# Perceiver layer on one core: the delta rule's heads projected before their norm factor is known

## The reference, cut to what matters

```python
core = gated_delta_rule(q, k, v, g, beta)                    # 8 heads, 128 tokens, 128 values
core = core * rsqrt(mean(core * core, -1) + EPS) * gate_norm_w
core = core * silu(z)                                        # z: one projection of x per head
h = resid + core.reshape(B, S, VAL_DIM) @ W_out              # VAL_DIM = 8 * 128, h has 256 columns
x = zrms(h, w_ln2)                                           # then router, gate, up, down
```

## Time and profile before

| | us |
|---|---|
| median of three runs | 228.49 |
| lowest and highest | 228.28, 228.62 |
| span of the profiled execution, first to last instruction | 226.6 |
| TensorE busy | 218.7 (97%) |
| VectorE busy | 143.6 (63%) |
| ScalarE busy | 145.2 (64%) |
| GpSimd busy | 133.8 (59%) |

### The profile page before, as it was taken

One profiled execution on the slowest core, in us unless ns is written; L12 is line 12 of the kernel. 1 busy time (PEld: TensorE's weight loads), 2 busy tenths in 40 slices (PEclk: granted clock), 3 DMA queues, 4 the chain that ended last, 5 costly groups with the idle time before them and its releaser, 6 DMA issues.

```text
span 226.6 us, 4199 instructions
## 1 busy us (share of the span) xinstructions
PE 218.7 (97%) x1555; PEld 194.3 (86%) x1555; DVE 143.6 (63%) x346; ACT 145.2 (64%) x264; POOL 133.8 (59%) x86
## 2 busy tenths in 40 slices
PE   8999999999999999989989999989999999999994
PEld 7747888888888888979879999876799999999993
DVE  2337666666666668656986776355225579788783
ACT  5258877777777779348876676782326758677570
POOL 1129888888898888831799956550002525555550
PEclk9999999999999999999999999999999999999999
DMA  6999999999999803999400000001980677960000
GB/s 214 400 425 419 420 418 415 405 418 420 421 414 420 368 8 123 425 343 410 189 3 1 1 3 0 3 0 17 382 346 13 216 330 286 396 246 0 3 0 23
DMA packets 8532, 52.94 MB, mean 234 GB/s; under 512 B 953, under 2 KB 1218, under 8 KB 6466
## 3 DMA queue, kind: packets, MB, share of 16 engines
q1 hardware_dynamic: 8514, 52.69, 58.4%
HBM read 52.56 MB, written 0.13 MB: 233 GB/s over the span
## 4 chain that ended last, share of the span: by engine, by line
PE 85%; DVE 7%; ACT 4%; issue 1%; POOL 1%; ACTq 0%; DVEq 0%; POOLq 0%
PE psum L501 28%; PE psum L581 13%; PE psum L845 8%; PE psum L496 7%; PE psum L557 6%; PE psum L492 3%; PE psum L713 3%; PE psum L726 3%; PE psum L756 2%; PE psum L796 1%; PE psum L598 1%; DVE ctxT_hi L1242 1%; ACT ring L1042 1%; PE psum L659 1%; DVE w_lo L1524 1%
## 5 line engine op out<-in xcount | busy, mean ns | idle before, releaser
L399 POOL TENSOR_TENSOR ctx_lo<-ring,ctx_hi 128x1792 fp32r<-128x1792 f32 x13 | 52.6, 4046 | 13.8 <-ACT ctx_hi L911 13.8
L484 POOL TENSOR_TENSOR h_lo<-ring,h_hi 128x512 fp32r<-128x512 f32 x16 | 24.7, 1546 | 45.1 <-ACT h_hi L1132 39.1
L501 PE MATMUL psum<-late_sb,work 128*128 128x448 f32 x68 | 27.8, 541 | 0.0
L501 PE MATMUL psum<-xT,late_sb 128*128 128x128 f32 x224 | 26.4, 276 | 0.1
L501 PEld LDWEIGHTS psum<-xT,late_sb 128*128 128x128 f32 x224 | 25.6, 192 | 0.3 <-DVE xT L1494 0.3
L911 ACT ACTIVATE ctx_hi<-ring 128x1792 fp32r<-128x1792 f32 x13 | 22.1, 1701 | 3.7 <-DMA ring<-in_ctx 3.7
L1192 DVE TENSOR_REDUCE smalls<-psum 128x1 f32<-128x896 f32 x14 | 15.3, 1092 | 14.4 <-PE psum L557 9.1
L918 ACT ACTIVATE probsT_hi<-psum 128x512 fp32r<-128x512 f32 (+1 forms) x26 | 12.7, 542 | 17.4 <-PE psum L496 17.4
L1216 DVE TENSOR_TENSOR probsT_lo<-psum,probsT_hi 128x512 fp32r<-128x512 f32 (+1 forms) x26 | 15.0, 619 | 6.6 <-ACT probsT_hi L918 6.6
L501 PEld LDWEIGHTS psum<-late_sb,work 128*128 128x128 f32 x68 | 11.9, 190 | 8.1 <-issue 7.8
L496 PE MATMUL psum<-early_sb,work 128*128 128x128 f32 x115 | 16.1, 273 | 0.2 <-ACT work L1080 0.2
(11 more groups left out here) (281 smaller groups left out, 513.7 us busy)
## 6 DMA issues: line engine op xcount, KB each, us to landing
late_sb<-in_ctx_T SPq DMA_DIRECT2D x14, 896.0 KB, 11.2
ring<-in_ctx SPq DMA_DIRECT2D x14, 896.0 KB, 9.9
late_sb<-in_late SPq DMA_DIRECT2D x10, 825.0 KB, 10.8
late_sb<-in_experts SPq DMA_DIRECT2D x8, 1024.0 KB, 6.2
late_slots<-in_experts SPq DMA_DIRECT2D x8, 1024.0 KB, 7.4
early_sb<-in_early SPq DMA_DIRECT2D x1, 512.0 KB, 3.7
early_sb<-in_early SPq DMA_DIRECT2D x1, 465.0 KB, 7.8
work<-in_levels SPq DMA_DIRECT2D x1, 416.0 KB, 9.5
```

The source lines that it names most:

```text
L399: nc.gpsimd.tensor_tensor(ctxNv[1][:, r % 2], ring[:, r], ctxNv[0][:, r % 2], ALU.subtract).then_inc(s["ctx_lo"], 1)
L484: nc.gpsimd.tensor_tensor(hT[1][:, e % 2, at, :], h32[:, at, :], hT[0][:, e % 2, at, :], ALU.subtract).then_inc(s["h_lo_done"], 1)
L501: last = nc.tensor.matmul(o, lhs(c), rhs(c), start=(c == 0), stop=(c == n - 1))
```

## The change

The factor `f` is no longer multiplied into the heads before the transpose. Each head is projected as it is, into a PSUM bank of its own (`Y_BANKS`), and VectorE multiplies with `f` while it sums the eight results, in two sums (even heads onto `h0` in `hh`, odd heads in `xn`), and adds the two at the end. The squares are taken behind `gate_output`, with eight accumulating ScalarE instructions. The copy of the first half's transposes goes to VectorE. The projections of gates 4 to 7 move: two behind the last convolution projection, one ahead of level 1, one into level 6; they go to `bank[6]`, and the column norms of `k` move from `bank[6]` to `bank[5]`. Eight `keep_warm` products go away. The diff, cut to its core:

```diff
@@ -25,7 +25,8 @@
-Z_GAPS = {2: 0, 3: 1, 4: 2, 5: 3}
+Z_GAPS = {2: 0, 3: 1, 4: 2, 5: 3, 6: 7}
+Y_BANKS = (0, 7, 1, 2, 3, 5, 4, 6)
@@ -248,6 +249,10 @@
+def head_out(h):
+    return bank[Y_BANKS[h]][:, 0:D]
@@ -642,7 +647,7 @@
-    last = wide(bank[5 if h < 4 else 2][:, h % 4 * P:(h % 4 + 1) * P], lambda c: half(xT, c),
+    last = wide(bank[5 + h // 4][:, h % 4 * P:(h % 4 + 1) * P], lambda c: half(xT, c),
@@ -677,6 +682,8 @@
+project_z(4)
+project_z(5)
@@ -690,6 +697,7 @@
+project_z(6)
@@ -737,33 +745,29 @@
-    pe.wait_ge(s["zs_done"], 1)
+    pe.wait_ge(s["zs_done"], b + 1)
...
+def core_transposes(b):
+    pe.wait_ge(s["zo_done"], b + 1)
+    transposes([(bank[3 + b][:, k * P:(k + 1) * P], core[:, 4 * b + k, :]) for k in range(4)], s["core_T"])
+def project_out(h):
+    nc.tensor.matmul(head_out(h), coreT[:, h, :], w_out[:, h, :], start=True, stop=True).then_inc(s["out_mm"], 1)
+core_transposes(0)
+core_transposes(1)
+pe.wait_ge(s["coreT_dve"], 1)
+for h in range(0, 4):
+    project_out(h)
+pe.wait_ge(s["osq_done"], 1)
+pe.wait_ge(s["coreT_act"], 1)
...
-    project_z(h)
-keep_warm(4)
-def core_transposes(b):
-    pe.wait_ge(s["core_dve"], b + 1)
-    if b == 0:
-        pe.wait_ge(s["core_act"], 1)
-    transposes([(bank[3 + b][:, k * P:(k + 1) * P], core[:, 4 * b + k, :]) for k in range(4)], s["core_T"])
-def project_out(heads):
-    pe.wait_ge(s["coreT_done"], heads[0] // 4 + 1)
-    for h in heads:
-        last = nc.tensor.matmul(bank[0][:, 0:D], coreT[:, h, :], w_out[:, h, :], start=(h == 0), stop=(h == HV - 1))
-    return last
-core_transposes(0)
-keep_warm(4)
-project_out(range(0, 1))
-core_transposes(1)
-project_out(range(1, 4))
-last = project_out(range(4, HV))
-last.then_inc(s["out_mm"], 1)
+    if h == HV - 1:
+        pe.wait_ge(s["osq_done"], 2)
+    project_out(h)
@@ -1064,29 +1068,23 @@
+silu_z(1)
...
-act.wait_ge(s["o_mm"], 1)
-nc.scalar.activation(squares[:, 0:4, :], bank[5][:, :].rearrange("p (h t) -> p h t", h=4), ACT.Square).then_inc(s["osq_done"], 1)
-act.wait_ge(s["o_mm"], 2)
-for k in range(4):
-    last = nc.scalar.activation(squares[:, 4 + k, :], bank[6][:, k * P:(k + 1) * P], ACT.Square, accum_out=s_("ms", 4 + k, 5 + k))
-last.then_inc(s["osq_done"], 1)
-silu_z(1)
-act.wait_ge(s["zo_done"], 1)
-act.wait_ge(s["f_done"], 1)
-nc.scalar.activation(core[:, 3, :], core[:, 3, :], ACT.Copy, scale=s_("f", 3, 4)).then_inc(s["core_act"], 1)
...
-    act.wait_ge(s["core_T"], b + 1)
-    nc.scalar.activation(coreT[:, 4 * b:4 * b + 4, :], bank[3 + b][:, :].rearrange("p (h t) -> p h t", h=4), ACT.Copy,
-                         scale=early_at("gate_norm")).then_inc(s["coreT_done"], 1)
-    if b == 0:
-        gate_up_hi(2)
+    act.wait_ge(s["zo_done"], b + 1)
+    for k in range(4 * b, 4 * b + 4):
+        last = nc.scalar.activation(squares[:, k, :], bank[5 + b][:, k % 4 * P:(k % 4 + 1) * P], ACT.Square, accum_out=s_("ms", k, k + 1))
+    last.then_inc(s["osq_done"], 1)
+act.wait_ge(s["core_T"], 2)
+nc.scalar.activation(coreT[:, 4:8, :], bank[4][:, :].rearrange("p (h t) -> p h t", h=4), ACT.Copy, scale=early_at("gate_norm"))\
+    .then_inc(s["coreT_act"], 1)
+gate_up_hi(2)
+gate_up_hi(3)
...
-gate_up_hi(3)
@@ -1412,35 +1411,38 @@
-    if b == 0:
-        link(V.tensor_reduce(s_("ms", 0, 4), squares[:, 0:4, :], AX, ALU.add))
...
+    dve.wait_ge(s["o_mm"], b + 1)
...
-def normalize(b, heads):
-    dve.wait_ge(s["zo_done"], b + 1)
-    dve.wait_ge(s["f_done"], b + 1)
-    for h in heads[:-1]:
-        V.tensor_scalar(core[:, h, :], core[:, h, :], s_("f", h, h + 1), None, ALU.mult).then_inc(s["dve_chain"], 1)
-        chain[0] += 1
-    h = heads[-1]
-    V.tensor_scalar(core[:, h, :], core[:, h, :], s_("f", h, h + 1), None, ALU.mult).then_inc(s["core_dve"], 1)
+gate_output(0)
+gate_output(1)
...
-gate_output(0)
+dve.wait_ge(s["core_T"], 1)
+V.tensor_scalar(coreT[:, 0:4, :], bank[3][:, :].rearrange("p (h t) -> p h t", h=4), early_at("gate_norm"), None, ALU.mult)\
+    .then_inc(s["coreT_dve"], 1)
...
-normalize(0, range(0, 3))
-gate_output(1)
-normalize(1, range(4, HV))
...
-dve.wait_ge(s["out_mm"], 1)
-V.tensor_tensor(hh[:, :], bank[0][:, 0:D], h0[:, :], ALU.add).then_inc(s["h_done"], 1)
+odd = xn
+for h in range(HV):
+    dve.wait_ge(s["f_done"], h // 4 + 1)
+    dve.wait_ge(s["out_mm"], h + 1)
+    f = s_("f", h, h + 1)
+    if h > 1:
+        dve.wait_ge(s["y_sum"], h - 1)
+    if h == 1:
+        V.tensor_scalar(odd[:, :], head_out(h), f, None, ALU.mult).then_inc(s["y_sum"], 1)
+    else:
+        total = hh if h % 2 == 0 else odd
+        V.scalar_tensor_tensor(total[:, :], head_out(h), f, h0[:, :] if h == 0 else total[:, :], ALU.mult, ALU.add).then_inc(s["y_sum"], 1)
+dve.wait_ge(s["y_sum"], HV)
+V.tensor_tensor(hh[:, :], hh[:, :], odd[:, :], ALU.add).then_inc(s["h_done"], 1)
```

More of the change, by code:

```diff
@@ L224, in perceiver @@
             tanh_kb k_done sq_done n2_done n2_read kn_in decay_done exp_decay dt_done gram_done aw_done vT_done bv_done
-            an_T x_done t_mm t_done xt_T xt_done xx_mm zt_mm za_done zb_done o_mm osq_done ms_done f_done core_dve core_act zo_done raw_v core_T coreT_done
+            an_T x_done t_mm t_done xt_T xt_done xx_mm zt_mm za_done zb_done o_mm osq_done ms_done f_done zo_done raw_v core_T coreT_dve coreT_act y_sum
             out_mm h_done hsd_done x2_done x2_T x2_copied x2_hi x2_lo gu_hi gu_lo lg_mm dm_in tanh_done gu_mm gact_done prod_done prod_T prodT_done
@@ L671, in _ @@
             pe.wait_ge(s["sq_done"], 1)
-            lengths(HK, bank[6])
+            lengths(HK, bank[5])
             pe.wait_ge(s["k_done"], 1)
@@ L1025, in silu_z @@
                 act.wait_ge(s["z_done"], b + 1)
-                nc.scalar.activation(zs[:, 4 * b:4 * b + 4, :], bank[5 if b == 0 else 2][:, :].rearrange("p (h t) -> p h t", h=4), ACT.Silu).then_inc(s["zs_done"], 1)
+                nc.scalar.activation(zs[:, 4 * b:4 * b + 4, :], bank[5 + b][:, :].rearrange("p (h t) -> p h t", h=4), ACT.Silu).then_inc(s["zs_done"], 1)
             def copy_xt(lv):
@@ L1347, in _ @@
             dve.wait_ge(s["n2_done"], 1)
-            V.tensor_scalar(s_("n2", HK, 2 * HK), bank[6][:, HK:2 * HK], 4 * RMS_EPS, None, ALU.add).then_inc(s["kn_in"], 1)
+            V.tensor_scalar(s_("n2", HK, 2 * HK), bank[5][:, HK:2 * HK], 4 * RMS_EPS, None, ALU.add).then_inc(s["kn_in"], 1)
             dve.wait_ge(s["kn_in"], 1)
-            link(V.reciprocal(bank[6][:, 0:HK], s_("n2", HK, 2 * HK)))
+            inverse = bank[5][:, 0:HK]
+            link(V.reciprocal(inverse, s_("n2", HK, 2 * HK)))
             link(V.tensor_tensor(s_("kap").rearrange("p (k r) -> p k r", r=2), s_("beta").rearrange("p (k r) -> p k r", r=2),
-                                 bank[6][:, 0:HK].rearrange("p (k r) -> p k r", r=1).to_broadcast([P, HK, 2]), ALU.mult))
+                                 inverse.rearrange("p (k r) -> p k r", r=1).to_broadcast([P, HK, 2]), ALU.mult))
             def decay_gram(h, other):
```

## The result

The changed kernel took 229.61 us at the median of 12 executions (228.29 to 231.44), the kernel before 228.76 on the same chip (228.01 to 229.07, also 12). The ratio, taken over all executions, is 1.0048, with a 95% interval of 1.0026 to 1.0070 (the two medians alone give 1.0037): slower by about half a per cent. The forecast was 228.4 with a range up to 228.9, so the result lies above the range, and on the side that had a chance of 0.12.

What follows compares the result with a forecast made beforehand. The 9.80 us from the first half's outputs to `h_done` were taken as the bound; 2.03 us gained unblocked shrank to 0.12 with the addition blocked, so 228.49 becomes 228.4, range 226.4 to 228.9.

Steps and rivals of the forecast that it cites:

- Projections and the path to the eighth product: Gates 4 to 7 in TensorE's gaps cost 0.25 us; the eighth head's sum ends at 146.39 before adding that.
- GpSimd and the blocked addition: VectorE's last addition waits for GpSimd's fourth remainder; `h_done` at 149.01 instead of 149.13, 0.12 us gained; chance 0.76.
- the 128x4 operation: VectorE's mean of squares, both inputs in SBUF, beside GpSimd's powers: expected not to wait, since one took 0.15 there.
- Behind `h_done` nothing changes: After the residual sum, the rest keeps its time; the table load and both remainders are done earlier than before.
- second rival: TensorE's clock falls to 1.2 GHz in the new 2.9 us wait, losing 1.9 us: 230.3 us; chance 0.06.
- the wait has work before and behind it: Argument against TensorE's clock falling in the new 2.9 us wait for `hh`.
- The start's sixteen products: First sixteen unread products on TensorE, 3.79 us at half speed; taken as the length of a clock fall.
- The first rival: VectorE's final addition is not blocked by GpSimd, gaining 2.03 us: 226.5 us; chance 0.14.

Runs made afterwards that it cites:

- e3: Changed kernel with the last sum of the odd heads written to a free part of a PSUM bank, GpSimd's order untouched: 226.47 us, ratio 0.9898 to the kernel before.
- e0: The changed kernel run again unedited: 230.65 us, ratio 1.0105 to the kernel before.
- e6: Kernel before, with VectorE's residual addition made to wait for GpSimd's fourth remainder: 232.36 us, ratio 1.0165 to the kernel before.
- e2: Changed kernel with GpSimd's fourth remainder held until `h_done`: 226.58 us, ratio 0.9905 to the kernel before.
- e1: Changed kernel with 24 unread products behind the eighth head's projection, in TensorE's wait for `hh`: 230.79 us, ratio 1.0095 to the kernel before.
- e5: Changed kernel with 12 unread products behind the eighth head's projection, in TensorE's wait for `hh`: 228.29 us, ratio 0.9995 to the kernel before.
- e7: Kernel before, with the residual addition waiting for GpSimd's fourth remainder and 11 unread products filling TensorE's wait: 230.84 us, ratio 1.0119.

## Why the prediction was wrong, point by point

**Projections and the path to the eighth product: right.** The forecast gave 0.25 us to the four projections. The outputs' gating starts at 139.59, and 139.58 is what it comes to with the 0.25 (140.01 + 0.25 less the 0.68 that it takes). Projection 7 moved level 6's second half by 0.21, where 0.20 was forecast. With 0.25 added, the squares were to start at 140.30, the mean at 141.51 and the heads on TensorE at 142.33; they did at 140.32, 141.50 and 142.37. VectorE's copy took 0.74 and not the 0.69 of ScalarE's. The eighth sum ended at 146.67, forecast 146.64. That these times agree to some hundredths leans on the two traces starting the stage level (97.25 and 97.20 us, and 134.60 and 134.62 in level 6).

**GpSimd and the blocked addition: right.** Remainders to 148.71, measured 148.78; the addition ends 0.28 behind them, forecast 0.30; `h_done` at 149.06, forecast 149.01; TensorE's wait 3.0 us, forecast 2.9. The profiled execution took 228.53, and the three at full clock have a median of 228.53 where 228.4 was forecast. The prediction weighed a rule of the Trainium skill (SBUF — State Buffer, Who interferes with whom): two SBUF inputs on VectorE collide with a GpSimd instruction that reads SBUF, while at most one doesn't, outside VectorE's two-port modes, of which no run here shows anything. By the runs it holds on both sides: two SBUF inputs beside GpSimd, 2.35 us; one SBUF input beside the same instruction in e3, 0.42. For the 128x4 operation the rule was doubted on rows 2 and 5, and the changed kernel again shows one of 0.16 us, at 142.53, within GpSimd's powers (141.74 to 143.79).

**The step that failed: "Behind `h_done` nothing changes".** It is true of the work behind `h_done`, and true of the time only at full clock. The prediction named the mechanism as its second rival, in the place where it happened, but gave it 0.06, against 0.76 for the same addition at full clock. Measured, 9 of 12 executions, and 6 of 6 in e0, were that rival. The argument against was "the wait has work before and behind it"; it does, and that doesn't protect it: e6 has work on both sides as well and falls in 5 of 5. The other half of the argument, that no slice of the profile before shows a lowered clock, had no weight either. The longest wait of TensorE behind the start was 0.6 us, so the trace of before held no case of the question. With one row pointing each way and none for a wait of 3 us, the two cases should have stood near even, and the range should have reached past 230.

The Trainium skill (TensorE: Matmul & The Clock Gate, HAM oscillation) warned that gaps in TensorE's work bring its clock back to half. The runs agree: behind the wait of 3.0 us the mean clock came out lower in 15 of 18 executions, and e0's trace shows it at half. The forecast had put the time in that case at 230.3.

**The size of the fall: half right.** The rival priced 3.8 us at half clock, 1.9 lost. In e0 the low stretch is 6.8 us and the rest grows by 2.5. That is less than half of 6.8: for the first 0.6 us of it TensorE still stood idle, and what makes up the remaining 0.6 was not traced. In e6 the rest grows by 2.7. In the changed kernel's own executions at 0.984 to 0.985 the median is 230.9, 2.4 above those at full clock, and in those at 0.992 to 0.993 it is 229.5, 0.9 above. The start's sixteen products were a poor measure for how long the clock stays low, and the profile's granted clock does not show their stretch at all: it stands at 1.00 from 0 to 6 us, while they take 0.237 us each. So 230.3 lies between the two groups more by luck than by its working.

**The first rival, the unblocked addition.** It did not happen in the changed kernel, but e2 and e3 make its condition true, and its price was right: 226.5 forecast, 226.58 and 226.47 measured.

So the change earned its two microseconds. They went, in this order, to an exclusion between VectorE and GpSimd, which alone makes it even with the kernel before, and to the clock, which makes it slower. What mean clock an execution gets, and so the distance from the range, stays open.

## What to carry to other kernels

When an edit only moves a wait, ask how long the bottleneck engine now stands still in one piece: three microseconds of TensorE idle cost another 1 to 2.5 us behind it in 15 of 18 executions here, while 1.1 us cost nothing, and unread products in the wait took the whole loss back. When two accumulators in SBUF are joined on the critical path beside GpSimd work, leave one of them in PSUM. Look at the mean clock of every execution and not only at the profiled one: the first profile here showed full clock and a time that most executions missed. And when a rival's price would leave the range and no row bears on its condition, its chance is not small, only unknown.

## What the runs showed of the hardware that was not expected

- After the same wait of 3.0 us the clock fell in 15 of 18 executions of the changed kernel (9 of 12, then 6 of 6), to two different means, about 0.993 and 0.985. By half clock over a span of 228 us these are some 3 and 7 us at the low level (0.007 and 0.015 of 228, doubled). What decides between staying, a short fall and a long one was not found: the profiles of the changed kernel caught one execution that stayed and one that fell long, and no trace shows a short fall. In e6, with 3.19 us of idleness, all five fell, four of them to 0.993.
- Unread products kept the clock up as real ones did: in e1, e5 and e7 it was 0.998 or more in all 23 executions.
- A blocked VectorE instruction comes out a little shorter behind GpSimd's end (0.28 us) than it takes alone (0.42). Between GpSimd's two remainders there is no gap for it: it became ready 0.3 us behind the start of the fourth. What happens to an addition that is already waiting when one GpSimd instruction follows another was not tried.
